# Fused adaLN block with differential attention on one core: norms one body ahead, step pieces in alternate units, maxima split before their transposes, output steps inside the last body

## The reference

```
mod = silu(c) @ wmod                    # six rows of 256 per batch: sa, ca, ga, sb, cb, gb
ga, gb = sign * max(abs, 0.25)
h = layernorm(x) * (1 + ca) + sa
q, k: 32 half-heads of width 8;  v: 16 heads of width 16
a = softmax(q1 k1) - lam * softmax(q2 k2), per head;  o = a @ v
o = o * rsqrt(mean(o*o) + 1e-5) * subln_w * (1 - LAMBDA_INIT), per head
x = x + ga * (o @ Wo.T)
h = layernorm(x) * (1 + cb) + sb
x = x + gb * (h @ ternary(weight).T * scale)
```

## Time and profile before

| | |
|---|---|
| median of three runs | 4042.49 us (4041.13 to 4048.74) |
| profiled execution | 4045.13 us, span 4043.3 us |
| PE busy | 3753.5 us (93%), 32082 matmuls |
| ACT busy | 3783.7 us (94%), of which exps 3763.0 |
| DVE busy | 1197.4 us (30%) |
| POOL busy | 634.0 us (16%) |
| first exp starts, last exp starts | 149.1 us, 3964.6 us |
| TensorE clock granted | 0.98 of full in the mean |

### The profile page before, as it was taken

How to read it: one execution, slowest core, us unless ns; L and a number is a source line. 1 busy time by engine, 2 the same in 40 slices (tenths; PEclk the granted TensorE clock), 3 DMA queues, 4 the chain that set the end, 5 groups by cost and what they waited for, 6 DMA issues and landing times.

```text
span 4043.3 us, 75625 instructions
## 1 busy us (share of the span) xinstructions
PE 3753.5 (93%) x32082; PEld 919.2 (23%) x32082; DVE 1197.4 (30%) x2826; ACT 3783.7 (94%) x4132; POOL 634.0 (16%) x401
## 2 busy tenths in 40 slices
PE   6699999999999999999989999999999999999996
PEld 3121212222122222222222222222221212222123
DVE  7322222223332322323423223232331212212124
ACT  1599999999999999999989999999999999999992
POOL 4111212111120210202012121211211010101000
PEclk8799999999999999999999999999999999999998
DMA  3302112210231313113130221313012121201202
GB/s 125 88 25 36 41 34 36 37 36 25 34 54 35 53 32 48 39 35 50 35 56 25 40 49 35 54 35 49 29 34 38 24 40 16 49 3 30 35 13 62
DMA packets 112430, 163.26 MB, mean 40 GB/s; under 512 B 18820, under 2 KB 86660, under 8 KB 111880
## 3 DMA queue, kind: packets, MB, share of 16 engines
q1 hardware_dynamic: 112072, 158.19, 20.6%
HBM read 97.82 MB, written 60.32 MB: 39 GB/s over the span
## 4 chain that ended last, share of the span: by engine, by line
ACT 62%; issue 19%; PE 11%; DVE 5%; POOL 2%; SPq 1%; DMA 1%; DVEq 0%; POOLq 0%; ACTq 0%
ACT probs L576 61%; PE ps L689 5%; PE ps L676 3%; PE ps L602 1%; DVE stats L814 1%; POOL seg_rs L549 1%; DVE normed L825 1%; PE ps L596 1%; DVE seg_t L948 1%; POOL a_rest L522 0%; POOL a_parts L524 0%; SPq L316 0%; POOL e_rstd L529 0%; DVE e_tmp L934 0%; DMA m_scr<-wmod_sb 0%
## 5 line engine op out<-in xcount | busy, mean ns | idle before, releaser
L576 ACT ACTIVATE probs<-ps 128x1024 f32<-128x1024 f32 x4096 | 3763.0, 1291 | 87.6 <-PE ps L676 86.0
L689 PE MATMUL ps<-probs,values 128*32 128x512 f32 x16384 | 2193.3, 607 | 26.3 <-DVE seg_t L948 16.9
L676 PE MATMUL ps<-queries,keys 64*128 64x512 bf16 x8192 | 1441.9, 386 | 152.6 <-DMA queries<-m_scr 24.7
L549 POOL TENSOR_TENSOR seg_rs<-seg_ms,neg_half 64x16 f32<-64x16 f32 x128 | 370.2, 2892 | 2582.1 <-DVE seg_ms L957 2582.1
L676 PEld LDWEIGHTS ps<-queries,keys 64*128 64x128 bf16 x8192 | 339.1, 93 | 1868.6 <-ACT probs L576 1723.2
L689 PEld LDWEIGHTS ps<-probs,values 128*32 128x32 f32 x16384 | 322.9, 108 | 654.3 <-issue 569.3
L948 DVE STREAM_TRANSPOSE seg_t<-ps 128x512 f32<-128x512 f32 x128 | 91.7, 716 | 1126.1 <-PE ps L689 1126.1
L959 DVE TENSOR_TENSOR seg_n<-seg_d,seg_rs 64x256 f32<-64x256 f32 x128 | 53.4, 417 | 386.2 <-POOL seg_rs L549 386.2
L596 PE MATMUL ps<-ident,normed 128*32 128x128 f32 x2048 | 103.0, 300 | 64.4 <-DVE normed L825 44.6
L910 DVE TENSOR_SCALAR a_qk<-ps 128x512 f32<-128x512 f32 x64 | 44.2, 691 | 331.6 <-PE ps L610 331.3
L934 DVE TENSOR_TENSOR e_tmp<-ps,e_gate 128x512 f32<-128x512 f32 x64 | 44.2, 691 | 330.3 <-PE ps L602 330.2
(11 more groups left out here) (118 smaller groups left out, 1203.2 us busy)
## 6 DMA issues: line engine op xcount, KB each, us to landing
queries<-q_scr SPq DMA_DIRECT2D x384, 64.0 KB
keys<-k_scr SPq DMA_DIRECT2D x384, 64.0 KB
v_scr<-a_v SPq DMA_DIRECT2D x128, 128.0 KB, 2.0
values<-v_scr SPq DMA_DIRECT2D x32, 512.0 KB
q_scr<-a_parts SPq DMA_DIRECT2D x32, 384.0 KB, 2.6
k_scr<-a_parts SPq DMA_DIRECT2D x32, 384.0 KB, 2.5
a_x<-in_x_dram SPq DMA_DIRECT2D x16, 512.0 KB, 4.6
attn_scr<-seg_o SPq DMA_DIRECT2D x128, 64.0 KB, 1.6
```

The source lines that it names most:

```text
L549: nc.gpsimd.tensor_tensor(seg_rs[:, :], seg_ms[:, :], neg_half[0:64, :], ALU.pow).then_inc(seg_rs_done, 1)
L576: nc.scalar.activation(probs[:, u % PRING, n % PAIRS, :, :], slots[slot_of(body, n)], ACT.Exp).then_inc(exp_done, 1)
L676: last = nc.tensor.matmul(slots[slot_of(body, n)][:, half, :], keys[buf][at:at + KS_ROWS, n % PAIRS, blk * P:(blk + 1) * P], queries[buf][ ...
L689: last = nc.tensor.matmul(pv[j:j + VW, :], values[buf][:, blk, half, :], probs[:, u % PRING, pair, half, :], start=(blk == 0), stop=(blk = ...
```

## The change

1. The unit of each piece comes from `steps_of(body)`. `spread(half)` puts the four pieces of a step in units 1, 3, 5 and 7 of a half segment of eight units, `close(first)` in four units in a row. Ordinary bodies use `spread` for all steps; turn bodies use `spread` for a-steps 0 to 5 and `close` for the rest.
2. `a_stats` and `a_apply` of the next body's chunk stand at unit 122 of the body before. `a_load` moves to segment 5, and the splits of q and k move to `SPLITS`.
3. The e-steps of batch 2 are all done in bodies 12 and 13, two chunks a body. Body 14 has no steps. In body 15 the two groups alternate by segment (`place_of`), so that a chunk of 512 tokens is complete behind every second segment; its e-steps are then taken within the body (`E_LAST`), 14 of 24, and the other ten (`TAIL_E`) behind it.
4. The maxima are split into three bf16 parts before the transposes (`maxima_split`, 128 partitions), and the transposes are then bf16 matmuls with 96 output partitions, a copy and a store for each of the four. The flag's step comes last.

```diff
--- before.py
+++ after.py
...
-    STEP_PIECES = {NB * (n // 2) + ((7 if n == 0 else 3), 11)[n % 2] + p: (n, p)
-                   for n in range(A_STEPS + E_STEPS) for p in range(PIECES)}
+    HALF = NB // 2
     M_BLOCKS = 3
     M_BOUNDS = -(-NB // M_BLOCKS)
-    M_STEPS = M_BOUNDS + 1 + NC
-
-
-    M_UNITS = {NB * 3 + 8: 0, NB * 3 + 9: 1, NB * 3 + 10: 2, NB * 4 + 8: 3, NB * 4 + 9: 4, NB * 4 + 10: 5,
-               NB * 5 + 8: 6, NB * 5 + 9: 7, NB * 6 + 8: 8, NB * 6 + 10: 9, NB * 7 + 3: 10}
+    M_STEPS = M_BOUNDS + NC + 1
+    CRIT = M_STEPS - 1
+    LAST = B * GP - 1
+
+    def spread(half):
+
+        return [HALF * half + 1 + 2 * p for p in range(PIECES)]
+
+    def close(first):
+        return [first + p for p in range(PIECES)]
+
+
+    A_TURN = [spread(k) for k in range(6)] + [close(3 * NB + 3), close(3 * NB + 8)]
+    E_TURN = [close(3 * NB + 13), close(4 * NB + 3), close(4 * NB + 12), close(5 * NB + 3), close(5 * NB + 12), close(6 * NB + 3)]
+    M_TURN = [4 * NB + 9, 4 * NB + 10, 4 * NB + 11, 5 * NB + 8, 5 * NB + 9, 5 * NB + 10] + [6 * NB + 8 + k for k in range(NC + 1)]
+
+    E_LAST = [[close(2 * NB + 11), close(3 * NB + 3), close(3 * NB + 11), close(4 * NB + 3), close(4 * NB + 8), close(4 * NB + 12)],
+              [close(5 * NB + 3), close(5 * NB + 8), close(6 * NB + 3), close(6 * NB + 7), close(6 * NB + 11), close(7 * NB + 0)],
+              [close(7 * NB + 7), close(7 * NB + 11)]]
+
+    def steps_of(body):
+
+        b, gp = body // GP, body % GP
+        turn = gp == GP - 1 and b < B - 1
+        at = {}
+
+        def put(kind, job, tables):
+            for i, units in enumerate(tables):
+                for p, u in enumerate(units):
+                    assert u not in at, (body, kind, i, u)
+                    at[u] = (kind, job, i, p)
+
+        if b < B - 1:
+            put("a", body + NC, A_TURN if turn else [spread(i) for i in range(A_STEPS)])
+            if b > 0:
+                put("e", body - GP, E_TURN if turn else [spread(A_STEPS + 1 + i) for i in range(E_STEPS)])
+        elif gp < 2:
+            put("e", (b - 1) * NC + 2 * gp, [spread(3 + i) for i in range(E_STEPS)])
+            put("e", (b - 1) * NC + 2 * gp + 1, [spread(9 + i) for i in range(E_STEPS)])
+        elif body == LAST:
+            for tc, tables in enumerate(E_LAST):
+                put("e", b * NC + tc, tables)
+        if turn:
+            for i, u in enumerate(M_TURN):
+                assert u not in at, (body, "m", i, u)
+                at[u] = ("m", b + 1, i, PIECES - 1)
+        return at
...
-    LAST_E = [(0, 0), (0, 1)]
-    for j in range(NC):
-        LAST_E += [(j, 2), (j, 3)] + ([(j + 1, 0), (j + 1, 1)] if j < NC - 1 else []) + [(j, 4), (j, 5)]
+    TAIL_E = [(NC - 2, i) for i in range(len(E_LAST[-1]), E_STEPS)] + [(NC - 1, i) for i in range(E_STEPS)]
     LAST_JOB = (B - 1) * NC
-    M_LINKS = 2 + 4 + M_BOUNDS + 1 + P_LINKS * NC
+
+    SPLITS = {1: (0,), 2: (1, 2), 3: (3,)}
...
+        def place_of(body, s):
+
+            return (s % 2, s // 2) if body == LAST else (s // NC, s % NC)
...
+            def m_stores(b):
+                for k in range(NC):
+                    sp.wait_ge(m_evacuated, b * M_STEPS + M_BOUNDS + k + 1)
+                    m_store(b, k, m_stored)
+                sp.wait_ge(m_stored, (b + 1) * (NC * DMA))
...
+                            if s == 4:
+                                a_store_v(body + NC, b + 1, gp)
+                            if s == 5 and body + 1 < (B - 1) * GP:
+                                if turn:
+                                    a_columns(b + 2)
+                                a_load((body + 1) // GP + 1, (body + 1) % GP)
+                            if s == 6 and turn:
+                                m_stores(b + 1)
+                                group_maxima(b + 1, 0, 0)
...
+                        elif body == LAST:
+                            if s in (2, 4, 6):
+                                sp.wait_ge(seg_stored, (body * SEGS + s) * DMA)
+                                e_loads(b, s // 2 - 1)
...
+                        if s == SEGS - 1 and body + 1 < (B - 1) * GP:
+                            a_power(body + 1 + NC)
...
+                    elif body == LAST and s in (3, 5, 7):
+                        e_power(LAST_JOB + (s - 3) // 2)
+                    pool.wait_ge(seg_ms_done, body * SEGS + s + 1)
+                    nc.gpsimd.tensor_tensor(seg_rs[:, :], seg_ms[:, :], neg_half[0:64, :], ALU.pow).then_inc(seg_rs_done, 1)
...
-                buf, tc, blk = u // UNITS, u // NB % NC, u % NB
+                (buf, tc), blk = place_of(body, u // NB), u % NB
...
+                        if u % NB == 0 and place_of(body, u // NB)[1] == 0:
+                            pe.wait_ge(group_loaded[place_of(body, u // NB)[0]], (body + 1) * (GROUP_LOADS * DMA))
...
+                        kind, job, i, p = steps[u]
+                        if before and (kind == "m" or p == 0):
+
+                            bkind, bjob, bi = before
+                            if bkind == "a":
+                                pe.wait_ge(a_evacuated, bjob * A_STEPS + bi + 1)
+                            elif bkind == "e":
+                                pe.wait_ge(e_evacuated, bjob * E_STEPS + bi + 1)
+                            else:
+                                pe.wait_ge(m_evacuated, bjob * M_STEPS + bi + 1)
+                        before = (kind, job, i)
...
+                            elif i == 2 and p == 0:
+                                pe.wait_ge(e_normed, job + 1)
...
+                if body == LAST and s == SEGS - 1:
+                    e_evacuate(LAST_JOB + TAIL_E[0][0], TAIL_E[0][1], (aux, pv)[TAIL_E[0][1] % 2])
...
+                    steps = steps_of(body)
+                    if body == 0:
+                        a_stats(NC)
+                        a_apply(NC)
                     for u in range(BODY):
-                        if maxima and u == NB * 3:
+                        if u == M_TURN[0] - 18 and gp == GP - 1 and b < B - 1:
                             link = m_prepare(b + 1)
-                        if maxima and u in M_UNITS:
-                            if M_UNITS[u] == M_BOUNDS + 1:
-                                dve.wait_ge(m_stored, (b + 1) * DMA)
-                            m_evacuate(link, b + 1, M_UNITS[u])
-                        if u in STEP_PIECES:
-                            n, p = STEP_PIECES[u]
-                            if p == PIECES - 1 and n < A_STEPS and steps:
-                                a_evacuate(body + NC, n, b + 1, gp)
-                            elif p == PIECES - 1 and n >= A_STEPS and outputs:
-                                e_evacuate(body - GP, n - A_STEPS, b - 1)
+                        if u in steps and steps[u][3] == PIECES - 1:
+                            kind, job, i, p = steps[u]
+                            if kind == "m":
+                                if i == M_BOUNDS:
+                                    dve.wait_ge(m_stored, job * (NC * DMA))
+                                m_evacuate(link, job, i)
+                            elif kind == "a":
+                                a_evacuate(job, i, job // NC, job % NC)
+                            else:
+                                e_evacuate(job, i)
+                        if u == BODY - 6 and body + 1 < (B - 1) * GP:
+                            a_stats(body + 1 + NC)
+                            a_apply(body + 1 + NC)
                         if u % NB == NB - 1:
                             segment(body, u // NB)
 
-            link = Chain(dve, e_chain, LAST_JOB * E_LINKS)
-            for k, (tc, i) in enumerate(LAST_E):
-
-                e_evacuate(LAST_JOB + tc, i, B - 1, (aux, pv)[k % 2], k, link, (e_x2, a_x)[tc % 2])
+            for tc, i in TAIL_E[1:]:
+                e_evacuate(LAST_JOB + tc, i, (aux, pv)[i % 2])
```

More of the change, by code:

```diff
@@ L411, in _ @@
                     rows_of(b, 0, 0, m_rows_loaded)
-                    m_store(b, exact_done, runs + 1, m_rows_loaded)
+                    wait_alone(sp, exact_done, runs + 1, sp_passed)
+                    for k in range(NC):
+                        m_store(b, k, m_rows_loaded)
                     wait_alone(sp, m_rows_loaded, (runs + 1) * (EXACT_LOADS * DMA) - 2 * DMA, sp_passed)
@@ L418, in _ @@
                     body = b * GP + gp
-                    ejob = body - GP
+                    turn = gp == GP - 1 and b < B - 1
                     group_rows(b, gp * 2 + 1, 1)
                     group_maxima(b, gp * 2 + 1, 1)
-                    if b > 0:
+                    if 0 < b < B - 1:
                         if gp == 0:
@@ L432, in _ @@
-                            if s == 3:
[L433 to L437, removed]
-                        if s == 6 and body == B * GP - 1:
-                            sp.wait_ge(e_evacuated, ejob * E_STEPS + 2)
-                            sp.wait_ge(seg_stored, (body * SEGS + s) * DMA)
```

(33 more changed lines are left out.)

246 lines of the change are left out of this document (112 added, 134 removed).

## The result

The changed kernel takes 4037.35 us (median of 15 runs, 4027.64 to 4043.89), the kernel before 4043.96 beside it (15 runs, 4041.13 to 4048.84): ratio 0.998, interval 0.9972 to 0.9988. So it is faster by 0.12 to 0.28%, and whether by more than the 0.2% named in the prediction stays open. The forecast was 4031. The profiled execution took 4034.29 us with a span of 4032.6, 10.7 less than the span before, where the sum gave 10.4 before rounding.

The account below looks back on a forecast made before the run. ACT's 4096 exps bound the kernel; gains of 73.8 us less costs of 63.4 gave net 10.4, rounded to 11.5, off a median of 4042.5: 4031 us, forecast range 4021 to 4041, wider range 4005 to 4050.

Parts of the forecast that it names:

- norm ahead: Unit 7 of bodies 1 to 11: norms one body ahead end PE's wait for `normed`, gaining 37.4 us.
- transpose behind the output norm: Twelve bodies with outputs: the segment transpose no longer queues behind the output norm chain, gaining 12 x 0.41 = 4.9 us.
- tail: Behind the last exp: 10 of 24 steps remain, end at 4011.8 instead of 4043.3, gaining 31.5 us (28 to 34).
- ten waits for `e_normed`: At output step 2, PE stands some 3.0 us; ten times 3.4 us costs 34 us (25 to 39).
- two turn bodies: Unit 67 of bodies 7 and 11: PE stands 6.5 us for step 0's evacuation; 7.2 each costs 14.4 us.
- last body's rows: Segment 1 of the last body waits for its second buffer's loads, costing 12 us (9 to 15).
- first output load of body 12: At unit 25, e_x lands 2 us after PE reaches the piece, costing 1.5 us (0 to 3).
- start: Before the attention: four stores of the maxima's parts instead of one cost 0.5 us (0 to 1.5).
- A: The ten `e_normed` waits cost near 0 to 1.7 us each, giving 3997 to 4021 us; chance 0.17.
- B: All costs at their upper ends, +12 to +15 us: 4043 to 4046, no change that can be told; chance 0.16.
- C: Slower: PE at half clock makes the ten `e_normed` waits 6.5 us each, 65 us, 4062 us; chance 0.11.
- D: Tail doesn't shrink because chunk 2 or its store delays chunk 3: 4042 us or more; chance 0.04.

Follow-up runs that it names:

- experiment 7: Kernel before with only the a-norms taken at unit 122 of the body before, their pow and load moved along: 4007.5 us, 0.9905 of the kernel before.
- experiment 3: Changed kernel with output step 2 of ordinary bodies begun one unit later, shortening the wait: 4004.51 us, 0.9914 of the kernel before.
- experiment 5: Changed kernel with a third buffer for the last body's second group, loaded in body 14: 4022.52 us, 0.9943 of the kernel before.
- experiment 8: Changed kernel with output step 1 packed, turn-body steps one unit earlier, third buffer, body 12's output loads ahead of rows: 3974.91 us, 0.9822 of before.
- experiment 1: Changed kernel with output step 1 of ordinary bodies in four units in a row: 4004.31 us, 0.9904 of the kernel before.
- experiment 2: Changed kernel with all steps of ordinary bodies in four units in a row: 4000.62 us, 0.9885 of the kernel before.
- experiment 4: Changed kernel with a-steps 6 and 7 and the output steps of turn bodies moved one unit earlier: 4019.33 us, 0.9947 of the kernel before.
- experiment 6: Changed kernel with body 12's output loads and modulation issued ahead of its second group's rows: 4033.82 us (10 runs), 0.9972 of the kernel before.

## Why the prediction was right, and where it was off

**The mechanism of each named step held.** The steps by their numbers:

| step | predicted us | measured us |
|---|---|---|
| norm ahead | -37.4 | -39.7 in the trace, -37.8 in experiment 7 |
| transpose behind the output norm | -4.9 | -6.0 |
| tail | -31.5 (28 to 34) | -34.7, by the pair of executions 29.7 to 34.7 (below) |
| ten waits for `e_normed` | +34 (25 to 39) | +35.8 |
| two turn bodies | +14.4 (up to 16.8) | +18.5 (19.8 less 1.3 before) |
| last body's rows | +12 (9 to 15) | +12.2 here, 6.8 to 12.2 over the six traces that have it |
| first output load of body 12 | +1.5 (0 to 3) | +4.0 here, 3.4 to 4.4 in four others |
| start | +0.5 (0 to 1.5) | +1.2 here, not separable from its spread (below) |
| close pairs in the last body | +1 | +2.2 |

*The sum came closer than its terms.* The gains came out at 80.4 us where 73.8 was worked out, the costs of the table at 73.9 where it was 63.4. Two errors of 6.6 and 10.5 us cancelled in part, and some 4 us more came from places that the prediction put at nothing: 1.4 in the first units of bodies 4, 8 and 12, and 2.8 in the rest, most of it in the turn bodies, where units beside pieces and bounds had lost 0.13 to 0.24 us each. So the net of 10.4, against 10.7 between the spans, owes part of its closeness to luck.

*The ten waits.* Length 2.96 us where 3.0 was worked out, cost 2.53 at full clock where 2.5 was taken, and 3.7 in seven bodies and 4.7 in one where 3.9 was. The clock fell in eight of ten, and behind unit 92, three units on, ACT loses nothing more. The Trainium skill (TensorE: Matmul & The Clock Gate, HAM oscillation) describes a loop in which the gap of every pass, longer than the one here, brings the array back to half rate. Here eight waits of 2.96 us do so and two of the same length do not, so the trace agrees only in part.

*The turn bodies* were the term most mis-sized. PE's wait was right (6.5 predicted, 6.69 measured). "At the wait's length less 0.5 that is 6.0; by body 8 ... it is 8.4. I take 7.2": ACT's first gap alone is 7.5 us longer than a usual one, because behind the wait PE must do the piece (1.08 us), then scores (1.04), both at half rate, where they usually take 0.61 each; and 1.8 to 3.0 us more follow until the slots are full again. The 8.4 of body 8 was the nearer row; even it was short.

*Body 12.* The lateness was 2.87 us, not 2. The landing was placed well (48.3 us behind the end of the body's first exp, where the rows gave 48.1: SP came to `e_x` 1.9 us later than before, and the transfer took 13.9 us and not 15.6). PE came to the piece at 45.4 instead of 46.1, mostly because the body's first unit lost 1.4 us less than before. The larger part of the error is the price: it was taken as the wait less a cover (1.5), without the clock's part. Here the clock fell (0.57 in the mean from 3067 to 3071 us), and 2.87 us cost 4.0.

*The tail.* Chunk 3 starts 18.3 us behind the place that 3967.31 had before (its last exp ended 1.2 us ahead of it; 3990.02 here), where 17.9 was worked out. From there to the end it took 23.0 us, and the sum had 26.6: 26.4 of before's last chunk, less 1.3 for DVE being shared, plus 1.5 for half clock. The 1.3 held. From the Wo products to the transposes it took 11.1 us before, where the transposes waited for an `e_y` of the chunk ahead, and 9.9 here. The clock went the other way than the 1.5. The last chunk's product with the ternary weight, before and after:

```profile
4032.59 5.83 PE L602 MATMUL ps<-w_f,e_hT 128*32 128x256 f32 x64 [0.93 <-DVE e_hT L931]
```
```profile
4024.01 3.66 PE L656 MATMUL ps<-w_f,e_hT 128*32 128x256 f32 x64 [0.93 <-DVE e_hT L977]
```

The granted clock was 0.50 from 4032 to 4036 us before and 1.00 from 4024 to 4028 here, and from the transposes to the end it took 15.3 and 13.1 us. These 2.2 us belong to the two executions and not to the change: in experiments 3, 5 and 8 the same product took 5.4 to 5.6 us and the whole tail 44.8 to 45.0, in the changed kernel and experiments 1, 2, 4 and 6 3.66 us and 42.6 to 43.1, and in experiment 7, which has the tail of before, 3.66 us and 74.6 instead of 77.3. Each tail shows both. So the tail's gain is 29.7 to 34.7 us by the pair that is compared, and the 34.7 in the table is its upper end.

*Why the medians differ by only 6.6 us* when the spans differ by 10.7: the profiled execution of before was 1.2 us above its median, the one of after 3.1 below. The changed kernel's 15 runs spread over 16 us, those of before over 8; the stall for the last body's rows, 6.8 to 12.2 us by how fast the transfers ran, is one part of that which before did not have.

**The rivals.** A (waits half as dear) is refuted by the slope in experiment 3. B (all costs upper) came true for two of four costs and was balanced by the tail. C (6.5 us a wait at half clock) did not happen: the mean was 3.6 and the dearest 4.7, below the 5.4 from which C would decide. D (tail does not shrink) is refuted by the tail's own rows. That the loss would move elsewhere when mended is refuted by experiments 1, 4, 5 and 8.

## What to carry to other kernels

When pieces of side work are spread more evenly over a loop, measure first whether their density costs anything (here nothing did in ordinary bodies, and 0.9 to 1.9 us in a turn body before the change), and then list the chains between consecutive steps: the gap between the last piece of one and the first of the next is what spreading uses up, and beyond the first 0.4 us every microsecond by which the chain is longer is paid about one for one. Where two engines run written-out orders, look for every place where a step straddles a block of the other engine (here four pieces across a segment's end: 19 us for one unit's shift). And price the parts of a combined change singly: one part of this one gave 37.8 us alone, the tail some 30 to 35 by the traces, and the four places that took 71.8 back were repaired by moving pieces and loads and by one more buffer.

## What the runs showed of the hardware

**The start is not the same in two executions.** The first exp started between 143.8 us (experiment 3) and 159.8 (experiment 2) over ten traces, though nothing ahead of it differs among the changed kernel and experiments 1 to 6. The windows of two of these kernels, experiment 5 and experiment 6, over the same 4 us (us, busy of PE, PEld, DVE, ACT, POOL, PEclk, DMA share, GB/s), and SP's waits for the maxima's store in the same two:

```profile
134.00:138.00 4.00, 0.00 (x0) 0.00 (x0) 0.00 (x0) 0.00 (x0) 0.00 (x0) 0.50 0.98 243
```
```profile
134.00:138.00 4.00, 0.00 (x0) 0.00 (x0) 0.00 (x0) 0.00 (x0) 0.00 (x0) 0.50 0.90 130
```
```profile
SPq L407 <- DMA m_scr<-wmod_sb: 5.8, 1, 5.8
```
```profile
SPq L396 <- DMA m_scr<-wmod_sb: 16.6, 1, 16.6
```

With the DMA engines 98% and 90% busy, one moved 243 GB/s and the other 130, and SP waited 5.8 or 16.6 us behind its issue of the four stores. What sets the rate of such an execution is open. From the first store's issue to the load behind the last took 7.7 us (experiment 5) to 18.4 (experiment 6) over the eight traces with four stores, and 12.1 and 15.1 in the two with one, so a cost of 6 us for the three more can't be told from this spread. The Trainium skill (DMA: Bandwidth & Descriptors, Anatomy of one DMA) gives a fixed cost of about 2 us for each DMA, on the path of GpSimd; here SyncE issues them. Paid in full one behind another, four such costs would be 8 us before any data is counted, an estimate from that figure, and the 7.7 of experiment 5 is less than that with the data in it.

**The same stand of PE has two prices.** The ten waits of 2.96 us left the granted clock at 1.00 twice (2.53 us lost) and lowered it eight times (3.7 us, once 4.7). Experiments 4, 5 and 6 have the same ten. Of the 40 waits, six left the clock at 1.00, and they lie in bodies 4 and 9 in the changed kernel, in 12 in experiment 4, in 9 in experiment 5, and in 5 and 12 in experiment 6. So it is not the place in the program that decides, and I found no row ahead of the waits that tells the two apart. Three of the 40 cost 4.7 to 4.9; there the clock fell 0.7 to 1.2 us before the wait was over. Of shorter waits, six of nine of 2.24 us lowered it in the kernel before, and none of ten of 1.1 us in experiment 3.
